# A fourth buffer for input bands, with doubled sums kept in the output staging and weights built in the sums' buffer

## What is computed

```python
def _L0_conv_ref(x, W_id, b_id, ...):
    res = conv3x3(x, W_id, b_id)               # all 8 images
    cA, cH, cV, cD = _swt2_level3(x[0])        # wavelet of the first image alone
    high = jnp.stack([cH, cV, cD], axis=1).reshape(1, C3, H, W)
    low_att = _attention(cA[None], DCT_LOW, W_dl, b_dl, W_al, b_al, W1_low, W2_low)
    high_att = _attention(high, DCT_HIGH, W_dh, b_dh, W_ah, b_ah, W1_high, W2_high)
    dmt = jnp.concatenate([low_att, high_att], axis=1)
    out = jax.nn.leaky_relu(conv3x3(dmt, W_enc, b_enc), 0.01)
    return out + res                           # one map is added to every image

x = x + _L0_conv_ref(_gn(x), ...)
```

## Time and profile before

| what | us |
|---|---|
| median of 3 timed runs (lowest, highest) | 1819.07 (1810.22, 1823.49) |
| the profiled execution | 1814.87 |
| its span, first to last instruction | 1813.1 |
| busy in the span: PE / DVE / ACT / POOL | 1761.4 / 1450.2 / 1238.6 / 545.5 |

### The profile page before, as it was taken

How to read it: one execution, slowest core, us unless ns; L and a number is a source line. 1 busy time by engine, 2 the same in 40 slices (tenths; PEclk the granted TensorE clock), 3 DMA queues, 4 the chain that set the end, 5 groups by cost and what they waited for, 6 DMA issues and landing times. The chain is left out here.

```text
span 1813.1 us, 69228 instructions
## 1 busy us (share of the span) xinstructions
PE 1761.4 (97%) x31540; PEld 1470.2 (81%) x31540; DVE 1450.2 (80%) x1926; ACT 1238.6 (68%) x1339; POOL 545.5 (30%) x365
## 2 busy tenths in 40 slices
PE   9999999999999999989999999999999999999997
PEld 9997999999999999965577797767966756967676
DVE  5665578778777887668989889888889888888886
ACT  5555666666666666667776777767776767766774
POOL 0005788888888888640000000000000000000000
PEclk9999999999999999999999999999999999999999
DMA  8884399888888888458998998998989989989994
GB/s 186 245 296 126 122 274 227 212 219 216 212 215 215 215 215 206 100 125 204 235 234 223 239 239 226 240 240 229 238 224 236 247 213 232 242 219 230 249 234 140
DMA packets 132964, 391.84 MB, mean 216 GB/s; under 512 B 49884, under 2 KB 50656, under 8 KB 118464
## 3 DMA queue, kind: packets, MB, share of 16 engines
q1 hardware_dynamic: 132672, 387.43, 82.7%
HBM read 258.88 MB, written 128.45 MB: 214 GB/s over the span
## 5 line engine op out<-in xcount | busy, mean ns | idle before, releaser
L1766 PE MATMUL ps<-big,tail 64*64 64x448 f16 x3840 | 323.3, 353 | 11.8 <-DVE ps L1961 7.8
L1766 PE MATMUL ps<-pool_of 64*64 64x448 f16 x5184 | 302.5, 352 | 7.9 <-DVE pool_of L1625 4.2
L1766 PE MATMUL ps<-pool_of,tail 64*64 64x448 f16 x4896 | 300.1, 349 | 0.7 <-issue 0.7
L1766 PE MATMUL ps<-big,pool_of 64*64 64x448 f16 x3552 | 278.5, 352 | 17.1 <-DVE ps L1961 11.9
L1292 DVE BATCH_NORM_STATS2 pool_of<-big 128x6 f32<-128x448 f32 x392 | 232.2, 616 | 76.4 <-DMA big<-in_x 76.3
L1766 PEld LDWEIGHTS ps<-pool_of 64*64 64x64 f16 x5184 | 196.2, 107 | 68.0 <-issue 10.1
L1766 PEld LDWEIGHTS ps<-pool_of,tail 64*64 64x64 f16 x4896 | 189.6, 106 | 59.3 <-issue 1.3
L1066 PE MATMUL ps<-pool_of 112*128 112x246 f16 x1344 | 218.8, 271 | 1.7 <-DVE pool_of L1280 0.8
L1070 PE MATMUL ps<-pool_of 112*128 112x168 f16 x1344 | 217.8, 243 | 0.0
L1766 PEld LDWEIGHTS ps<-big,tail 64*64 64x64 f16 x3840 | 169.0, 107 | 57.9 <-DVE ps L1961 10.4
L1069 PE MATMUL ps<-pool_of 112*128 112x90 f16 x1344 | 201.3, 206 | 0.0
(11 more groups left out here) (252 smaller groups left out, 3809.8 us busy)
## 6 DMA issues: line engine op xcount, KB each, us to landing
out<-tail SPq DMA_DIRECT2D x448, 224.0 KB, 3.6
big<-in_x SPq DMA_DIRECT2D x392, 224.0 KB, 5.2
pool_of<-in_x SPq DMA_DIRECT2D x139, 560.0 KB, 7.4
tail<-in_x SPq DMA_DIRECT2D x69, 560.0 KB, 7.4
pool_of<-row_filtered SPq DMA_DIRECT2D x110, 224.0 KB, 4.0
row_filtered<-big SPq DMA_DIRECT2D x2, 6272.0 KB, 22.8
pool_of<-in_x SPq DMA_DIRECT2D x30, 392.0 KB, 7.1
row_filtered<-big SPq DMA_DIRECT2D x4, 1568.0 KB, 9.2
```

The source lines that it names most:

```text
L1766: mm = pe.matmul(psum[bank + r][C * k:C * k + C, 0:NT], wt[i % 2][lanes, h, s, kx, :], v[u][lanes, rows_of(k), kx:kx + W], start=False, st ...
```

## The change

It raises XS to 4. The fourth slot lies in `pool_of`, where `base` and `twice` were. `twice` moves into `stage[1]`, into the columns of the odd rows; `double` therefore waits for the stores of the minimal band before, and `odd_rows` for `seed_odd`. `made` moves into `sums`; `build_part` goes ahead of `neighbour_sums` and waits until the sums have been split. `base` is cut in two: three sets lie in `early`, three are made in the new slot and copied by GpSimd (`keep`) to where `made` was, before load 3 may overwrite them (`first_kept`).

```diff
-XS = 3
+XS = 4
...
             sp.wait_ge(conv_done, 2 * NE)
             ahead.load(sp, 2)
+            ahead.first_kept(sp)
+            sp.wait_ge(map_done, NE)
+            ahead.load(sp, 3)
...
             both_rows(NE - 1)
+            pool.wait_ge(conv_done, 2 * NE)
+            ahead.keep(pool)
...
-        xs = [pooled(0, RH * W), pooled(RH * W, RH * W), carve(RH * W)]
-        base = pooled(2 * RH * W, SET_N).rearrange("p (s k e) -> p s k e", s=NSET, k=3)
-        twice = pooled(2 * RH * W + SET_N, 4 * W).rearrange("p (r n) -> p r n", r=2)
+        xs = [pooled(0, RH * W), pooled(RH * W, RH * W), carve(RH * W), pooled(2 * RH * W, RH * W)]
...
-        first_made = sums[:, 0:TMP_N].rearrange("p (s k e) -> p s k e", s=NSET // 2, k=3)
+        made = sums[:, 0:TMP_N].rearrange("p (s k e) -> p s k e", s=NSET // 2, k=3)
...
-        made = carve(TMP_N).rearrange("p (s k e) -> p s k e", s=NSET // 2, k=3)
+        base = [v.rearrange("p (s k e) -> p s k e", s=NSET // 2, k=3) for v in (early[:, V_N + HI_N:V_N + HI_N + TMP_N], carve(TMP_N))]
+        early_base = xs[3][:, 0:TMP_N].rearrange("p (s k e) -> p s k e", s=NSET // 2, k=3)
+        twice = stage[1][:, :, :, W:NT]
...
+        def keep(pool):
+
+            pool.tensor_copy(base[1].rearrange("p s k e -> p (s k e)"), early_base.rearrange("p s k e -> p (s k e)")).then_inc(kept, 1)
+
+        def first_kept(sp):
+            sp.wait_ge(kept, 1)
+            sp.wait_ge(building, 11)
...
-            load(sp, 3)
-            load(sp, 4)
+            load(sp, XS)
+            load(sp, XS + 1)
...
-                load(sp, 2 * q + 5)
-                load(sp, 2 * q + 6)
+                load(sp, 2 * q + XS + 2)
+                load(sp, 2 * q + XS + 3)
...
                 act.wait_ge(m2_done, j + 1)
                 if j:
                     act.wait_ge(b_seeded, j)
-                act.activation(twice, a_bank, ACT.Identity, scale=-2.0, bias=lane(mean_r2, i)).then_inc(twice_ready, 1)
+                    act.wait_ge(stored[1], 64 * j)
+                act.activation(twice, a_bank.rearrange("p r (g w) -> p r g w", g=2), ACT.Identity, scale=-2.0, bias=lane(mean_r2, i)).then_inc(twice_ready, 1)
...
             def odd_rows(j):
                 i, b = minimal(j)
                 dve.wait_ge(odd_done, j + 1)
-                if j:
-                    dve.wait_ge(stored[1], 64 * j)
+                dve.wait_ge(b_seeded, j + 1)
...
                 if q >= 0:
                     diffs_low(q)
+                i, b = direct(q + 1) if q + 1 < ND else (B, 0)
+                if i + 1 < B and b in DIRECT[2:4]:
+                    dve.wait_ge(sums_split, q + 1)
+                    build_part(dve, i + 1, DIRECT.index(b) - 2)
                 if q + 1 < NW:
                     neighbour_sums(q + 1)
-                i, b = direct(q + 1) if q + 1 < ND else (B, 0)
-                if i + 1 < B and b in DIRECT[2:4]:
-                    build_part(dve, i + 1, DIRECT.index(b) - 2)
```

More of the change, by code:

```diff
@@ L81 @@
 Link = namedtuple("Link", "cleared einv_ready b32_in act_rows dve_rows first_split emx emax_part emax_all spread_max sx stat_in unit")
-Ahead = namedtuple("Ahead", "load weights_load dummies pads norms spread build normed high full split edges root partners sets spread_rows clear first_seed conv_first conv_rest")
+Ahead = namedtuple("Ahead", "load weights_load dummies pads norms spread build normed high full split edges root partners sets keep first_kept spread_rows clear first_seed conv_first conv_rest")
 def input_transform():
@@ L1450, in main @@
     with ExitStack() as s5:
-        tail = sb(s5, "tail", [P, RH * W + 4 * NT * 2 + V_N + SET_N + TMP_N])
+        tail = sb(s5, "tail", [P, RH * W + 4 * NT * 2 + V_N + SET_N + SET_N // 2])
         late = [0]
@@ L1482, in main @@
         inv, m_out, r_out, v_one, v_half, v_neg, neg_two, mean, mean_r, mean_r2 = [lanes_of[:, C + B * k:C + B * k + B] for k in range(10)]
-        diag = early[0:C, RH * W:RH * W + B * C].rearrange("p (i e) -> p i e", i=B)
+        diag = early[0:C, V_N:V_N + B * C].rearrange("p (i e) -> p i e", i=B)
         r_rows = pooled(AT_R, B * C).rearrange("p (i e) -> p i e", i=B)
@@ L1543, in main @@
         building = sem(top, "building")
-        built = sem(top, "built")
+        kept = sem(top, "kept")
         TOP, BOTTOM = 0, NB - 1
@@ L1715, in of @@
             def of(s):
-                return base[:, s, :, :].rearrange("p k e -> p (k e)")
+                return (base[0], early_base)[s // 3][:, s % 3, :, :].rearrange("p k e -> p (k e)")
             pool.wait_ge(weights_in, 48)
@@ L1724, in sets @@
             step(pool.tensor_scalar(of(3), of(3), 0.5, None, ALU.mult))
+        def keep(pool):
[3 more added lines that the diff above has]
+            sp.wait_ge(building, 11)
         def build_part(dve, i, h):
             n = 10 * i + 1 + 5 * h
-            v = made if i else first_made
+            v = made
             flat = v.rearrange("p s k e -> p (s k) e")
@@ L1732, in build_part @@
                 dve.wait_ge(sets_made, 6)
+            if i == 1 and h == 1:
+                dve.wait_ge(kept, 1)
             dve.wait_ge(building, n)
-            dve.tensor_tensor(flat, base[:, 3 * h:3 * h + 3, :, :].rearrange("p s k e -> p (s k) e"),
+            dve.tensor_tensor(flat, (base[h] if i or h == 0 else early_base).rearrange("p s k e -> p (s k) e"),
                               r_rows[:, i, :].unsqueeze(1).broadcast_to((P, 9, C)), ALU.mult).then_inc(building, 1)
@@ L1921, in neighbour_sums @@
                 k = place_w(j)
+                if j:
+                    dve.wait_ge(sums_split, j)
                 landed(dve, k)
@@ L1960, in seed_odd @@
                     dve.wait_ge(odd_read, 2 * j)
-                dve.tensor_tensor(b_bank, a_bank, twice, ALU.add).then_inc(b_seeded, 1)
+                dve.tensor_tensor(b_bank.rearrange("p r (g w) -> p r g w", g=2), a_bank.rearrange("p r (g w) -> p r g w", g=2), twice, ALU.add).then_inc(b_seeded, 1)
             def odd_rows(j):
@@ L2032, in main @@
                       normed=lambda act: act.wait_ge(normed, 1), high=high, full=full, split=split, edges=edges, root=root_of, partners=partners,
-                      sets=sets, spread_rows=spread_rows, clear=clear, first_seed=first_seed, conv_first=conv_first, conv_rest=conv_rest)
+                      sets=sets, keep=keep, first_kept=first_kept, spread_rows=spread_rows, clear=clear, first_seed=first_seed, conv_first=conv_first, conv_rest=conv_rest)
         return Programs(sync, tensor, scalar, vector, gpsimd), ahead
```

6 lines of the change are left out of this document (3 added, 3 removed).

## The result

| | us |
|---|---|
| median before, 4 runs (lowest, highest) | 1817.56 (1810.22, 1823.49) |
| median after, 4 runs (lowest, highest) | 2041.41 (2036.43, 2042.78) |
| ratio, with its 95% interval | 1.1229 (1.1182 to 1.1276) |
| the profiled execution after, and its span | 2042.68, 2040.9 |

What follows compares the result with a forecast made beforehand. TensorE set the pace before; now the doubling's wait for stores would: 11.75 + 9.6 + 0.1 = 21.45 us a turn against 17.76. Steps 1184.1 against 976.7, +207.5 on 1814.9: 2022 us, 8 in 10 for 1955 to 2080.

Steps and rivals of the forecast that it cites:

- the ring: In the loop, the doubling waits for the minimal band's stores and its lateness delays the next stores: 21.45 us a turn.
- doubling to first issue: From ScalarE's doubling through VectorE's gapless chain to the first store issued on SyncE: 11.75 us.
- issue of the eight: SyncE issuing the direct band's four stores and the minimal band's four in one row: 6.0 us, 5.56 to 7.05.
- landing after the last issue: Time until the block's last store, one of the minimal band's, has landed: 3.6 us, 2.8 to 6.0.
- the turn: One loop step from doubling to doubling: 21.45 us against 17.76 before, bounds 20.25 and 22.5.
- The first step: First to second doubling: 21.45 us plus 7 for a first store delayed behind three loads, 28.45 us.
- The clock's cover: TensorE's half clock after each wait, 1.7 us of lost work, fits before the minimal band's stores can be issued.
- Its rival: TensorE becomes the bound through half clock, 1 to 2 us more a turn, 2076 to 2130 us; chance 0.05.
- The store does not land fast: Denies the rival that issue and landing take only four stores' time, 6.1 us, giving 1830 us; chance 0.03.
- Not slower: Rival at the doubling (L1879): the stores have landed when wanted, within 7.35 us of first issue; 1815 to 1822 us, chance 0.05.
- Stores land later still: Rival: loads issued right behind the stores share the DMA engines; above 22.5 us a turn, 2082 to 2150, chance 0.07.
- The costs put at nothing: Fourth slot, building in the sums' buffer, runs of 224 and odd_rows' changed wait: each taken as 0 us.

Runs made afterwards that it cites:

- with the clock at 0.99: The changed kernel with 72 more matmuls of zero weights per turn ahead of product_m1, where TensorE waits for the doubling: 2039.60 us, ratio 1.1208.
- a kernel made for it: The changed kernel with both loads of a turn held back until that turn's split: 2164.72 us, ratio 1.1905.

## Why the prediction was right

The forecast was 2022 us in a range of 1955 to 2080; the time is 2041.41. What carried it is the ring, and its terms can be measured one by one over the 53 ordinary steps:

| term | forecast | measured mean (range) |
|---|---|---|
| doubling to first issue | 11.75 | 11.81 (46 turns 11.76 to 11.77) |
| issue of the eight | 6.0 | 6.26 (5.75 to 7.35) |
| landing after the last issue | 3.6 | 3.54 (2.61 to 4.87) |
| wake-up of ScalarE | 0.1 | 0.11 |
| the turn | 21.45 | 21.72 (20.7 to 23.2) |

**What was mis-sized.** The issue, by 0.26 us: the forecast took the middle one of 53 blocks of before, where the sum wants a mean, 6.14, and in the change it is 0.12 more. With the other terms the turn is 0.27 us longer, which make 14.3 us in 53 steps. The first step is 30.54 instead of 28.45: the three loads had landed at 831.75 and the store at 834.64, where the forecast had 827 and 831. Why they took longer was not tested; a fourth load was issued at 823.59, before they had landed. VectorE's wait for a load, up to 827.39, adds nothing to that, as it stands for the store behind it anyway. The last step is 19.34 instead of 18.8. That is 17.0 us together, and with 1.7 before the first doubling and 1.7 behind the last one it is the whole of the 20.3 between forecast step sum plus unchanged ends and the profiled execution. The end's 1.7 had been taken as unchanged.

**Where luck helped.** The 3.6 us of the earlier trace rows count from the start of an issue, over all stores, but the sum adds them to the end of the last issue. The last store of a block lands 4.4 us after its own start, before and after the change; its issue takes 0.9 of that, and 3.5 are left. So two errors nearly cancel. First issue to last landing was 9.70 us in the mean of before, and could have been read from its trace as it was.

**What the waits showed.** TensorE waits for the doubling in each turn, as forecast; 2.9 us instead of 3.7, because it also works longer. The doubling itself waits 4.8 instead of the 3.5 to 4.5 given, as ScalarE has nothing to do from 1108.27 on and stands ready. The DMA share is 0.74, as forecast. `seed_odd` is still named 21 times, with 0.42 us in the middle one, and one of 8.4 us in the first turn, at 839.28, behind VectorE's wait for the store; the 2.0 us stalls are gone. A wait on a load, a sign of being wrong, stands there once, the 3.83 us of the first turn, and in no turn behind it. The steps are nearly, not quite, the same in all turns: seven have 12.1 to 12.35 to the first issue.

**The clock's cover held.** TensorE's wait in this turn, and the stretches behind it (columns as in the earlier trace rows):

```profile
1113.86 0.57 PE L1781 MATMUL ps<-big,tail 64*64 64x448 f16 x8 [3.32 <-ACT tail L1895]
```

```profile
1113.86:1115.00 1.14, 1.14 (x24) 0.72 (x28) 0.00 (x0) 1.14 (x1) 0.00 (x0) 1.00 0.94 228
1115.00:1118.40 3.40, 3.40 (x45) 1.68 (x40) 2.35 (x1) 3.40 (x3) 0.00 (x0) 0.51 0.56 126
1118.40:1124.00 5.60, 5.60 (x124) 3.33 (x120) 5.60 (x5) 1.59 (x3) 0.00 (x0) 0.99 0.79 182
```

Behind the wait of 3.3 us the clock stays at 2.4 GHz for 1.1 us, is at 1.2 GHz for 3.4 us, some 1.7 us of work lost, and comes back; a mean of 0.94 in the loop is 0.06 x 1201 = 72 us lost. The low clock stands in 38 of the 55 turns. The rule of the Trainium skill that the prediction named (TensorE: Matmul & The Clock Gate, HAM oscillation — how this bites in real kernels) tells of a low clock that returns with each wait, and this trace agrees in those 38 turns only. But it costs nothing here: with the clock at 0.99 the time was 2039.60. Its rival falls, as it was priced.

**The other rivals.** The store does not land fast: first issue to landing is 8.85 us at the least, where it would have had to be 6.1. *Not slower* fell with it. The estimate of 6.2 from the Trainium skill (DMA: Bandwidth & Descriptors, Anatomy of one DMA — SWDGE (gpsimd) path) is not borne out: the fit given there is for one DMA issued by GpSimd, and here SyncE issues eight, one by one. *Stores land later still* is real, but not from the loads issued behind the stores, as that rival put it: it comes from loads issued ahead of them, and only a kernel made for it went beyond the range's end.

**The costs put at nothing.** The building alone measured 0.9998; slot and building together leave the steps within 0.06 us of those of the doubled sums alone; the fourth slot shows no gain over the doubled sums alone (the late start aside), nor over the kernel with three slots and the building earlier. It was not run without the doubled sums in a staging buffer. `keep` took 0.66 us, less than the 1.13 at the least that were given. That the slot could pay in a kernel where loads are waited for was not tried, as the loop of the kernel before waits for none.

## What to carry to other kernels

A buffer lent out between a DMA's issue and its next use is free only until someone else wants it: count from the first issue of the whole block to its last landing, set that against the moment when the new user stands ready, and look whether the user's lateness makes the next issue late, because then the sum is a ring and is paid in every turn. Where a buffer must be shared, take the one whose transfers are issued first (18.3 us a turn against 21.7 here), and look who waits for the ones that are now last. Work without a due time belongs into a wait that its engine has anyway: the four or five instructions of a building, moved ahead of one that waits, gave 26 us in 14 turns.

## What the runs showed of the hardware

- Stores issued 6 us behind two loads (four DMAs of 560 KB) landed 6.9 us after their issue in the median, up to 8.5 in the loop; with the loads spread as in the change, 3.6, up to 5.6. A loop with a mean DMA share of 0.63 was slowed by its DMAs: in the 9.4 us of a turn that counted the share was 1.00.
- Half clock in TensorE in 38 of 55 turns, a mean of 0.94, was worth less than the runs can tell (2041.41 against 2039.60 us), where TensorE waits in each turn for a ring that it is not part of.
- TensorE's waits that no semaphore explains come to 5.7 us in the loop of the change, 42.2 with two loads right behind each block of stores and short turns, and 46.2 with the loads later. In all twelve traces each of them ends 1.2 to 1.75 us after a packet of the instruction queue has ended. What makes them more frequent stays open.
